# Routing of the last batch in a cross-attention and mixture-of-experts kernel: one power for both scales, empty rows by direct transfers, first tiles with waits of their own

## What is computed

```python
x = x + tanh(g_xattn[3]) * L3_xattn(_layernorm(x), ctx, ctx, ...)
x = x + tanh(g_ffn[3]) * L3_ffn(_layernorm(x), ...)

def _L3_ffn_ref(x, gate_w, rms_w, W1, W2, W3):      # E, K = 8, 2; DM, DE = 256, 704
    y = _rmsnorm(x, rms_w)
    logits = jnp.einsum('bsd,ed->bse', y, gate_w)
    vals, idx = jax.lax.top_k(logits, K)
    w = jax.nn.softmax(vals, axis=-1)
    ...                                             # silu(y W1) * (y W2), then W3, of each chosen expert
    return x + comb
```

## Time and profile before

| | us |
|---|---|
| median of three runs | 2874.17 |
| lowest, highest | 2871.24, 2880.59 |
| the profiled execution's own time | 2873.16 |
| its span, first to last instruction | 2871.4 |
| turn 7 of the last attention stage | 27.60 |
| from x_all complete to the first expert product | 83.66 |
| the expert stage from there on | 597.63 |

### The profile page before, as it was taken

How to read it: one execution, slowest core, us unless ns; L and a number is a source line. 1 busy time by engine, 2 the same in 40 slices (tenths; PEclk the granted TensorE clock), 3 DMA queues, 4 the chain that set the end, 5 groups by cost and what they waited for, 6 DMA issues and landing times. The chain is left out here.

```text
span 2871.4 us, 39420 instructions
## 1 busy us (share of the span) xinstructions
PE 2469.6 (86%) x13988; PEld 1626.5 (57%) x13988; DVE 1392.8 (49%) x3132; ACT 891.6 (31%) x2000; POOL 552.2 (19%) x538
## 2 busy tenths in 40 slices
PE   4994399999999896896999889968885499999998
PEld 2442277666666564443656655434454277777776
DVE  4896565574445544785232543355763223222232
ACT  1221155544444442332232212223442022222222
POOL 1110222243001001212231000002246311111111
PEclk8997699999999998997999669989986699999999
DMA  5000300121001002000000000002015221222221
GB/s 175 1 1 24 105 16 8 45 81 59 23 23 45 23 27 79 1 1 15 0 0 0 32 21 0 0 3 110 16 53 203 90 33 32 34 34 33 32 34 27
DMA packets 73505, 110.46 MB, mean 38 GB/s; under 512 B 11608, under 2 KB 62680, under 8 KB 71520
## 3 DMA queue, kind: packets, MB, share of 16 engines
q1 hardware_dynamic: 41184, 66.45, 6.7%
q0 software_dynamic: 16752, 27.29, 4.8%
q10 hardware_dynamic: 15408, 14.50, 1.8%
HBM read 72.41 MB, written 37.01 MB: 38 GB/s over the span
## 5 line engine op out<-in xcount | busy, mean ns | idle before, releaser
L1684 PE MATMUL PS<-mem,ctx2T 128*128 x1136 | 350.9, 462 | 2.0 <-ACT ctx2T L1741 1.2
L1684 PEld LDWEIGHTS PS<-mem,ctx2T 128*128 128x128 f32 x1136 | 211.8, 191 | 109.1 <-issue 4.9
L308 POOL TENSOR_TENSOR rstd<-var_eps,minus_half 128x4 f32<-128x4 f32 x50 | 50.9, 1018 | 888.6 <-DVE var_eps L265 505.6
L1810 DVE TENSOR_TENSOR ctx2T<-PS,ctx2T 128x352 f32<-128x352 f32 x142 | 74.5, 525 | 268.4 <-PE PS L1684 268.4
L1850 POOL DMA_INDIRECT out_x<-xnT,moe_small x71 | 110.7, 1560 | 488.3 <-ACT xnT L1755 488.3
L1706 PE MATMUL PS<-mem,moe_small 128*128 x852 | 195.7, 379 | 1.1 <-DVE moe_small L1818 1.1
L1706 PEld LDWEIGHTS PS<-mem,moe_small 128*128 128x128 f32 x852 | 156.4, 190 | 19.9 <-issue 1.4
L895 DVE RECIPROCAL mem<-PS 128x512 f32<-128x512 f32 x48 | 160.8, 3351 | 13.9 <-PE PS L599 13.9
L890 DVE TENSOR_REDUCE mem<-PS 128x32 f32<-128x2048 f32 x48 | 109.9, 2291 | 80.2 <-PE PS L561 80.2
L2484 DVE TENSOR_REDUCE moe_small<-PS 128x2 f32<-128x1024 f32 x64 | 78.5, 1226 | 139.4 <-PE PS L2132 139.4
L2293 ACT ACTIVATE mem<-PS,moe_small 128x512 f32<-128x512 f32 x128 | 86.8, 683 | 157.1 <-DVE moe_small L2484 157.1
(11 more groups left out here) (340 smaller groups left out, 4608.9 us busy)
## 6 DMA issues: line engine op xcount, KB each, us to landing
mem<-in_L_ffn_experts SPq DMA_DIRECT2D x8, 2176.0 KB, 13.9
xn<-unit_rows SPq DMA_DIRECT2D x15, 512.0 KB, 4.1
xn<-slots ACTq DMA_DIRECT2D x53, 130.0 KB, 2.1
x_all<-in_x SPq DMA_DIRECT2D x8, 512.0 KB, 10.2
mem<-unit_rows SPq DMA_DIRECT2D x8, 512.0 KB, 3.9
out_x<-x_all ACTq DMA_DIRECT2D x8, 512.0 KB, 3.0
mem<-slots ACTq DMA_DIRECT2D x18, 130.0 KB, 2.1
unit_rows<-xn SPq DMA_DIRECT2D x4, 512.0 KB, 2.8
```

Of the source, the lines that this page charges most:

```text
L1684: last = nc.tensor.matmul(PS[:, 1 + 2 * g + half, 0:HE], m.rowT[:, j % 2, k, :], w[:, :, at:at + HE], start=k == 0, stop=k == KD - 1)
```

## The change

In TensorE's list project_out takes one tile of 128 rows instead of two. In the stages without rotation (L1 and L3) the waits for free banks stand ahead of the second scores of keys; in L1 the first tile of the projection, in L3 the transposes of y stand there too. In L3 the first tile comes ahead of turn_max. Four of the five products of ranks become one: VectorE adds the picks of four neighbouring tiles first (m.pairs, m.summed). On ScalarE ratios and copy_yT stand ahead of the second exponentials. Of the twelve operations of the scales one power over 128x8 is left on GpSimd (norm_powers); five are on VectorE, three of them (norm_scales) behind add_out, for the last batch ahead of all else in its turn. row_ends is done one turn before its scatter. GpSimd waits, ahead of the last batch's scatter, until all earlier ones have landed, and adds to the new semaphore rows_here; it does so again when all have landed and the empty rows too. These go out as eight direct transfers of ScalarE. The table is made in two parts, the first for 8 tiles, with an entry `needs` for each: 1, if all 128 of its rows were placed before the last batch, else 2. ScalarE waits for rows_here to reach it before it loads the tile.

```diff
@@ xattn_pe
-    def project_out(b, half):
+    def project_out(b, t):
         pe.wait_ge(s.sems["o_ready"], KD * (b + 1))
-        for t in (2 * half, 2 * half + 1):
-            for f in range(KD):
-                last = nc.tensor.matmul(PS[:, BANK_M + 1 - half, (t % 2) * D:(t % 2 + 1) * D], s.o[:, b % 2, f, t * P:(t + 1) * P],
-                                        s.wo[:, f, :], start=f == 0, stop=f == KD - 1)
-        last.then_inc(s.sems["y_psum"], 1)
+        for f in range(KD):
+            last = nc.tensor.matmul(PS[:, BANK_M + 1 - t // 2, (t % 2) * D:(t % 2 + 1) * D], s.o[:, b % 2, f, t * P:(t + 1) * P],
+                                    s.wo[:, f, :], start=f == 0, stop=f == KD - 1)
+        if t % 2 == 1:
+            last.then_inc(s.sems["y_psum"], 1)
...
-        for d in range(1, TB + 1):
-            last = nc.tensor.matmul(out, e.const("ones"), m.picked[:, (TB - d) * NE:(2 * TB + 1 - d) * NE],
-                                    start=False, stop=d == TB)
+        last = nc.tensor.matmul(out, e.const("ones"), m.summed[:, (TB - 1) * NE:2 * TB * NE], start=False, stop=True)
...
+        def banks_free():
+            if n + 1 < B:
+                if s.rope:
+                    pe.wait_ge(s.sems["swap_read"], KD * (n + 2))
+                else:
+                    pe.wait_ge(s.sems["q_ready"], KD * (n + 2))
+            else:
+                wait_for(pe, e.x_updated, s.x_before + TB * min(n - 2, B) if n > 2 else 0)
+
+        if not s.rope:
+            banks_free()
+            if route or rank:
+                wait_for(pe, m.sems["lr_ready"], lr_turn(n - 1))
+            if route:
+                turn_y(n - 4)
+            if old and not s.front:
+                project_out(n - 2, 0)
         if before:
             scores_of_keys(n - 1, 1, min(2 * n + 2, 2 * B))
-        if n + 1 < B:
-            if s.rope:
-                pe.wait_ge(s.sems["swap_read"], KD * (n + 2))
-            else:
-                pe.wait_ge(s.sems["q_ready"], KD * (n + 2))
-        else:
-            wait_for(pe, e.x_updated, s.x_before + TB * min(n - 2, B) if n > 2 else 0)
-        if s.front and (route or rank):
-            wait_for(pe, m.sems["lr_ready"], lr_turn(n - 1))
-        if route:
-            turn_y(n - 4)
-        if now:
-            turn_max(n)
+        if s.rope:
+            banks_free()
         if route or rank:
             if route:
                 last = logits(n - 4)
             if rank:
                 last = ranks(n - 5)
             last.then_inc(m.sems["lr_psum"], 1)
+        if old and s.front:
+            project_out(n - 2, 0)
+        if now:
+            turn_max(n)
         if old:
-            for half in range(2):
-                if half == 1 and now and not s.front:
-                    pe.wait_ge(s.sems["maxT_ready"], n + 1)
-                if half == 1 and (route or rank):
-                    pe.wait_ge(m.sems["lr_ready"], lr_turn(n))
-                project_out(n - 2, half)
+            if s.rope:
+                project_out(n - 2, 0)
+            project_out(n - 2, 1)
+            if now and not s.front:
+                pe.wait_ge(s.sems["maxT_ready"], n + 1)
+            if route or rank:
+                pe.wait_ge(m.sems["lr_ready"], lr_turn(n))
+            project_out(n - 2, 2)
+            project_out(n - 2, 3)
@@ xattn_act
-        act.wait_ge(m.sems["norm_ready"], b + 1)
+        act.wait_ge(m.sems["norm_ready"], 3 * (b + 1))
...
+        if rank:
+            ratios(n - 5)
         if before:
+            if route:
+                copy_yT(n - 4)
             exponentials(n - 1, 1)
-        if route:
+        elif route:
             copy_yT(n - 4)
+        if route or rank:
+            copy_lr(n)
         if now:
             copy_max(n)
         if m and n + 2 < B:
             apply_norm(n + 2)
-        if route or rank:
-            copy_lr(n)
-        if rank:
-            ratios(n - 5)
@@ xattn_dve
+        if b == B - 1:
+            order.mark(dve.tensor_copy(m.ahead, m.next))
+            order.settle()
...
+    def shares(b):
+        dve.wait_ge(m.sems["ratio_ready"], b + 1)
+        wait_for(dve, m.sems["meta_ready"], b - 1)
+        order.mark(dve.tensor_scalar(m.share[:, b % 2, :], m.ratio[:, b % 2, :], 1.0, None, ALU.add))
+        order.settle()
+        dve.reciprocal(m.share[:, b % 2, :], m.share[:, b % 2, :]).then_inc(m.sems["share_ready"], 1)
...
-        dve.tensor_tensor(m.picked[:, TB * NE:2 * TB * NE], m.pick[:, 0, :], m.pick[:, 1, :], ALU.add).then_inc(m.sems["picked"], 1)
+        order.mark(dve.tensor_tensor(m.picked[:, TB * NE:2 * TB * NE], m.pick[:, 0, :], m.pick[:, 1, :], ALU.add))
+        order.settle()
+        order.mark(dve.tensor_tensor(m.pairs[:, TB * NE:], m.picked[:, TB * NE:2 * TB * NE], m.picked[:, (TB - 1) * NE:(2 * TB - 1) * NE], ALU.add))
+        order.settle()
+        dve.tensor_tensor(m.summed[:, TB * NE:], m.pairs[:, TB * NE:], m.pairs[:, (TB - 2) * NE:(2 * TB - 2) * NE], ALU.add)\
+            .then_inc(m.sems["picked"], 1)
...
+        order.settle()
+        wait_for(dve, m.sems["norm_rstd"], b)
+        order.mark(dve.tensor_scalar(m.var[:, 0, :], m.mean_var[:, :, 1], LN_EPS, None, ALU.add))
+        order.settle()
+        dve.scalar_tensor_tensor(m.var[:, 1, :], m.var[:, 0, :], 1e-6, m.mean_var[:, :, 1], ALU.mult, ALU.add)\
+            .then_inc(m.sems["norm_var"], 1)
+
+    def norm_scales(b):
+        par = b % 2
+        dve.wait_ge(m.sems["norm_rstd"], b + 1)
+        wait_for(dve, m.sems["residual"], TB * (b - 1))
+        dve.scalar_tensor_tensor(m.shift[:, par, :], m.mean_var[:, :, 0], -1.0, m.scale[:, par, :], ALU.mult, ALU.mult)\
+            .then_inc(m.sems["norm_ready"], 1)
+        dve.scalar_tensor_tensor(m.res_shift[:, par, :], m.mean_var[:, :, 0], m.minus_gate, m.rstd[:, par, 0, :], ALU.mult, ALU.mult)\
+            .then_inc(m.sems["norm_ready"], 1)
+        dve.tensor_scalar(m.res_scale[:, par, :], m.rstd[:, par, 0, :], s.gate_out, 1.0, ALU.mult, ALU.add)\
+            .then_inc(m.sems["norm_ready"], 1)
...
+        if norm and n >= B + 2:
+            norm_stats(n - 3)
+            norm_scales(n - 3)
...
-        if norm:
+        if norm and n < B + 2:
             norm_stats(n - 3)
+        if rank:
+            shares(n - 5)
         if old:
             add_out(n - 2)
+        if norm and n < B + 2:
+            norm_scales(n - 3)
@@ xattn_pool
+    def norm_powers(b):
+        pool.wait_ge(m.sems["norm_var"], b + 1)
         wait_for(pool, m.sems["residual"], TB * (b - 1))
-        mean, var = m.mean_var[:, :, 0], m.mean_var[:, :, 1]
-        order.mark(nc.gpsimd.tensor_scalar(m.minus_mean, mean, -1.0, None, ALU.mult))
-        step(nc.gpsimd.tensor_scalar(m.rstd, var, LN_EPS, None, ALU.add))
-        step(nc.gpsimd.tensor_tensor(m.rstd, m.rstd, e.minus_half[:], ALU.pow))
-        order.mark(nc.gpsimd.tensor_scalar(m.res_scale[:, par, :], m.rstd, s.gate_out, 1.0, ALU.mult, ALU.add))
-        order.mark(nc.gpsimd.tensor_tensor(m.minus_mean, m.minus_mean, m.rstd, ALU.mult))
-        step(nc.gpsimd.tensor_tensor(m.ms, m.rstd, m.rstd, ALU.mult))
-        order.mark(nc.gpsimd.tensor_scalar(m.res_shift[:, par, :], m.minus_mean, s.gate_out, None, ALU.mult))
-        step(nc.gpsimd.tensor_tensor(m.ms, m.ms, var, ALU.mult))
-        step(nc.gpsimd.tensor_scalar(m.rrms, m.ms, 1e-6, None, ALU.add))
-        step(nc.gpsimd.tensor_tensor(m.rrms, m.rrms, e.minus_half[:], ALU.pow))
-        order.mark(nc.gpsimd.tensor_tensor(m.scale[:, par, :], m.rstd, m.rrms, ALU.mult))
-        step(nc.gpsimd.tensor_tensor(m.shift[:, par, :], m.minus_mean, m.rrms, ALU.mult))
-        pool.sem_inc(m.sems["norm_ready"], 1)
+        nc.gpsimd.tensor_tensor(m.rstd[:, b % 2, :, :].rearrange("p c t -> p (c t)"), m.var.rearrange("p c t -> p (c t)"),
+                                m.minus_half, ALU.pow).then_inc(m.sems["norm_rstd"], 1)
...
+        pool.wait_ge(m.sems["meta_ready"], b + 1)
...
+        if norm and n >= B + 2:
+            norm_powers(n - 3)
         if place:
-            row_ends(n - 6)
+            if n - 6 == B - 1:
+                all_scattered(pool, m, B - 1)
+                pool.sem_inc(m.rows_here, 1)
             scatter(n - 6)
-        if norm:
-            norm_scales(n - 3)
+        if norm and n < B + 2:
+            norm_powers(n - 3)
+        if rank:
+            row_ends(n - 5)
@@ moe_sync, moe_pe, moe_act
-    all_scattered(sp, s.front)
+    all_scattered(sp, s.front, B)
...
+        if j == FIRST_TILES:
+            pe.wait_ge(s.sems["tiles_ready"], 2)
...
-    act.wait_ge(s.sems["tiles_ready"], 1)
-    all_scattered(act, f)
-    act.wait_ge(s.padded_s, 16 * NE)
 
     def load(j):
+        if j < FIRST_TILES:
+            needs = act.value_load(s.needs[0:1, j:j + 1], min_val=1, max_val=2)
+            act.wait_ge(f.rows_here, needs)
+            act.sem_inc(e.spare, 1)
+        if j == FIRST_TILES:
+            act.wait_ge(s.sems["tiles_ready"], 2)
```

(24 more changed lines are left out.)

65 lines of the change are left out of this document (34 added, 31 removed).

## The result

The kernel after took 2852.07 us, the median of 5 runs (2850.65 to 2856.17), beside 2872.16 for the kernel before on the same chip: a ratio of 0.9925, with a 95% interval of 0.9911 to 0.9939. The forecast was 2848 us, the range 2836 to 2862. The time lies inside, 4 us above the forecast.

A forecast was written before the change was run, and what follows sets the result against it. Bounds: TensorE's gaps and own instructions in the last attention turns, then a chain of latencies before the expert stage. From 2873.16: turns win 15.0, second attention stage loses 1.8, turn 9 to first product wins 12.5; forecast 2848 us, range 2836 to 2862.

The forecast's parts named there:

- Turns 2 and 3: Last attention stage: a projected tile fills TensorE's 2.5 us wait for the reciprocal, 1.9 us won.
- These 14.0 us go, and what is late next is TensorE itself: Turns 4 to 8: TensorE's waits for copies of y, maxima, reciprocal and xnT vanish, leaving TensorE the late one.
- term (b): VectorE's added sums and scale operations ahead of the maxima make it late in turn 7 alone, 0.8 us lost.
- term (a): Norm's scales on VectorE behind add_out make xnT later; TensorE waits 1.35 us in turns 4 to 6, 4.0 lost.
- Turn 9: ratios ahead of copy_yT waits for VectorE's difference and delays the logits; less the ranks' saving, 1.7 us longer.
- its last transfer landed 11.22 us after its issue: scatter(4), amid four expert loads: starting 1.0 us later, it was to make normalised(7) start 1.0 later.
- Do the first tiles wait for less?: Start of expert stage: tile 0, two rows and padding, waits for everything and is first in queue; nothing won.
- Rival 1: Tile 0 early because expert 0 gets no row: expert stage starts 5.4 us earlier, 2842 us; chance 0.13.
- I take the quiet value, as one load is in flight and not four: Tile 0's row load beside the last expert's load: landing taken as 2.5 us, not 11.22.
- rival 3: GpSimd's wait ahead of scatter(7) or load 0's landing costs 11.2 instead of 2.5: 2856 us; chance 0.13.
- Rival 2: Reordered turns don't pay, VectorE or ScalarE being late instead: 6 won, 2857, or nothing, 2862 us; chance 0.20.
- Rival 4: Slower than before: expert stage's first tiles stay at 1.2 GHz, 4.7 us a tile, 2880 after seven; chance 0.04.

The follow-up runs named there:

- the second pair: The kernel before and the kernel after, both unchanged, traced once more on another chip: 2877.65 and 2848.29 us, one run each.

## Why the prediction was right or wrong, point by point

- **Turns 2 and 3**: 1.9 forecast, 1.7 measured. Right.
- **Turns 4 to 8**: 13.1 forecast, 14.7 and 13.9 measured (two pairs of traces). The sum is right by luck: its working is not. "These 14.0 us go, and what is late next is TensorE itself" failed: idle time fell by 3.5 us, where the terms say 8.0. VectorE and ScalarE are late next, with 5.2 us ahead of the first scores of keys (term (b) had 0.8), 3.9 in turn 8 (no term, nor had the 2.4 that stood there before), and 3.7 for xnT (term (a) had 4.0: right). What made up for it is a term that the sum did not have: the clock. TensorE's busy time fell by 11.2 us, 5 of them the ranks, as forecast and as the experiment on them shows; the other 6 are the same products at a higher clock (0.87 to 0.92 in the two rows above, 0.90 to 0.94 in the second pair). Which part of the change raised the clock stays open: the order of the transposes alone gave 1.4 us of busy time in the kernel before.
- **Second attention stage**: 0.3 a turn forecast, 0.35 measured; the 1.45 us that turn 8 gives back, by the clock, were missed. The stage costs about 0.7 us, not 1.8.
- **Turn 9**: 1.7 longer forecast, 2.3 measured, 2 of them the place of ratios. Right.
- **scatter(4) and normalised(7)**: the step that failed is "its last transfer landed 11.22 us after its issue", carried over as a fixed price. The landing is tied to the end of the four loads, 28 us behind x_all. In after the scatter starts 5.5 us behind the loads' issue and not 7.3, so the price was 13.8. Counted from x_all, normalised(7) came 1.4 us later than forecast and scatter(6) 0.9 later (40.3 us instead of 39.4).
- **The empty rows**: hidden, as forecast. The eight took ScalarE 7.9 us, 1.0 each, where 1.15 were forecast. The floor for a value load that the prediction cites does not hold here: in the kernel before the 0.47 us of the trace are the longest of the 71 of that line, and their median is 0.29 us.
- **Do the first tiles wait for less?** No, as forecast, and for the reason given: taking the part back changed 0.1 us, making tile 0 early won 8.3 beyond the 5.5 of the moved load. Rival 1 was false on the chip as in the reference.
- **The row load of tile 0**: "I take the quiet value, as one load is in flight and not four" failed. It took 7.93 us, not 2.5, and cost 5.5. This was half of rival 3; its other half, GpSimd's wait ahead of scatter(7), was harmless at 1.07 us. The Trainium skill, DMA: Bandwidth & Descriptors, Queues, rings and completion order, says that an engine takes turns between queues packet by packet. By that I had held the load for hardly disturbed. The trace does not agree with what I made of it: 2.1 us without the expert's load, 7.9 beside it. Whether the rule itself or my use of it fails, no run here shows.
- **Rival 2** (the turns don't pay) was nearer than its 0.20 and its prices say. VectorE was indeed the late one; it was the clock that paid.
- **Rival 4** (the clock stays down) did not come: the second group of 16 records took 5.00 us, as before.

Together: turn 9 to the first product won 5.3 us instead of 12.5, 7.2 less (5.5 the row load, 0.9 scatter(6), 0.6 turn 9); turns 4 to 8 won 1.6 more and the expert stage 1.3, and the small terms lost 0.3. That is the miss of 4.6 us against the profiled execution. In the turns two errors cancelled: 5 us too much of idle time, 6 too little of busy time. That the total came so near is luck to this extent, and a second trace of the same kernel can differ by 3 us in these turns by the clock alone.

## What to carry to other kernels

A transfer that the critical path waits for should not meet a bulk load that nobody needs yet: hold the bulk load back by a semaphore of later work. Here five loads moved by 78 us or more cost 0.9 us in the expert stage at most and gave 15.7. The price that the prediction read off a landing amid other transfers was not a duration but the distance to the end of those transfers, and it moved when they moved.

Where TensorE swings between two clocks, idle time has a second price in busy time, but no fixed one: 11.8 us of idle time came with 11.7 us of busy time in one comparison here, 4.8 with 1.4 in another, and in the change itself 3.5 with 6. So cost such a term as a range, and compare the granted clock and the busy time of each stretch before you believe a sum that comes out right.

The condition on "all rows of a tile have been placed" was decided here by a group of two rows, since it came first in the queue; look at what the first in order needs, not at the many behind it.

## What the runs showed of the hardware that I had not expected

- A row load of 130 KB took 2.1 us alone and 7.9 to 8.3 us beside one load of 2.2 MB on another queue; the loads of the experts took 8.4 to 9.6 us when one at a time.
- The same instructions in turn 4 took 27.49 us at a mean granted clock of 0.88 in one trace of after and 25.12 at 1.00 in another; single runs of one kernel spread from 2838.5 (clock 0.932) to 2851.6 (0.925).
- On one of the three chips that the experiments ran on, ScalarE and VectorE stood still for 2 to 9 us at a time in the routing turns, for nothing that the trace names. The cause is open.
- GpSimd's power over 128x8 took 1.68 us, over 128x4 1.05: less than twice.
